# A chunked linear-attention layer: half of the product with V moved between the projections of k and v, all masks put ahead of the root, and the last step's gate taken in halves with another root

## The reference

```
xn = layernorm(x)
q, k, v = silu(xn Wq), silu(xn Wk), silu(xn Wv)
# lightning attention in chunks, D = exp(ld * lag) where lag >= 0
scores  = (q k^T) * D
o       = scores v + (q S) * q_decay
S_new   = chunk_decay * S + (k * k_decay)^T v
# gate and norm over each head of 16
o       = o * sigmoid((xn Wg1) Wg2)
o       = o * rsqrt(mean(o*o over the head) + 1e-5) * norm_w
s       = o Wo
g       = silu(fp8(xn * scale) fp8(W2 * scale1) / (scale * scale1))
out     = x + s * g
```

## Time and profile before

| | |
|---|---|
| median of 3 runs | 127.22 us (126.68 to 128.17) |
| the profiled execution's own time | 126.63 us |
| its span in the profile | 124.9 us |
| TensorE busy | 114.0 us (91%) |
| VectorE, ScalarE, GpSimd busy | 97.6, 85.1, 89.8 us |
| granted TensorE clock | full speed in all 40 slices |

### The profile page before, as it was taken

One profiled execution on the slowest core, in us unless ns is written; L12 is line 12 of the kernel. 1 busy time (PEld: TensorE's weight loads), 2 busy tenths in 40 slices (PEclk: granted clock), 3 DMA queues, 4 the chain that ended last, 5 costly groups with the idle time before them and its releaser, 6 DMA issues.

```text
span 124.9 us, 6418 instructions
## 1 busy us (share of the span) xinstructions
PE 114.0 (91%) x2694; PEld 100.2 (80%) x2694; DVE 97.6 (78%) x263; ACT 85.1 (68%) x163; POOL 89.8 (72%) x124
## 2 busy tenths in 40 slices
PE   3969989998999999999999899999999999896890
PEld 3969989867988899779987698889988998774770
DVE  1799999999895999759894968689956993395862
ACT  7589989989996757666776576685874486831200
POOL 6826599979999796949968894969692988240440
PEclk9999999999999999999999999999999999999999
DMA  2669910011000400042002400051004214000213
GB/s 85 201 179 295 327 40 3 5 26 26 5 5 8 82 0 5 0 94 84 0 8 54 119 5 5 8 136 32 5 5 97 76 18 116 5 5 5 78 49 127
DMA packets 11084, 7.57 MB, mean 61 GB/s; under 512 B 4848, under 2 KB 11056, under 8 KB 11056
## 3 DMA queue, kind: packets, MB, share of 16 engines
q1 hardware_dynamic: 11056, 7.17, 20.9%
HBM read 3.50 MB, written 2.10 MB: 45 GB/s over the span
## 4 chain that ended last, share of the span: by engine, by line
PE 69%; DVE 16%; issue 5%; ACT 4%; DMA 3%; SPq 1%; DVEq 0%
PE b_o L1281 8%; PE b_q L1113 5%; PE b_s L1211 5%; PE b_kv L1126 5%; PE b_kv L1127 5%; PE b_kv L1129 5%; PE b_q L1343 3%; PE b_o L1261 3%; PE b_kv L1192 3%; PE b_q L1235 3%; DMA ld_row<-in_L_attn_log_decay_dram 3%; PE b_x L1305 2%; PE b_q L1118 2%; PE b_s L1182 2%; PE b_s L1166 2%
## 5 line engine op out<-in xcount | busy, mean ns | idle before, releaser
L1126 PE MATMUL b_kv<-w_hi,xT_hi 128*128 128x256 f32 x64 | 16.6, 283 | 0.0
L1127 PE MATMUL b_kv<-w_lo,xT_hi 128*128 128x256 f32 x64 | 16.4, 280 | 0.0
L421 POOL TENSOR_TENSOR e_sum<-e_y,e_magic 128x512 f32<-128x512 f32 x8 | 10.3, 1288 | 8.0 <-DVE e_magic L784 7.8
L833 DVE SCALAR_TENSOR_TENSOR og<-gate_tanh,b_o 128x512 f32<-128x512 f32 x7 | 4.8, 686 | 12.2 <-PE b_o L1281 12.2
L459 POOL TENSOR_TENSOR y<-sg,x_sb 128x512 f32<-128x512 f32 x7 | 9.0, 1291 | 6.6 <-DVE sg L932 6.6
L1129 PE MATMUL b_kv<-w_hi,xT_lo 128*128 128x256 f32 x64 | 12.7, 280 | 0.0
L1281 PE MATMUL b_o<-probs,v_par 64*32 64x64 f32 x896 | 12.4, 223 | 0.0
L1126 PEld LDWEIGHTS b_kv<-w_hi,xT_hi 128*128 128x128 f32 x64 | 12.1, 189 | 0.2 <-issue 0.2
L1127 PEld LDWEIGHTS b_kv<-w_lo,xT_hi 128*128 128x128 f32 x64 | 12.1, 189 | 0.0
L470 POOL TENSOR_TENSOR on_lo<-on,on_hi 128x512 fp32r<-128x512 f32 x6 | 7.7, 1281 | 5.8 <-ACT on_hi L651 5.8
L426 POOL TENSOR_TENSOR e_q<-e_sum,e_magic 128x512 bf16<-128x512 f32 x8 | 10.8, 1348 | 0.5
(11 more groups left out here) (211 smaller groups left out, 378.7 us busy)
## 6 DMA issues: line engine op xcount, KB each, us to landing
out_dram<-y SPq DMA_DIRECT2D x7, 256.0 KB, 2.8
x_sb<-in_L_attn_x_dram SPq DMA_DIRECT2D x4, 384.0 KB, 6.0
own_cross<-own_end SPq DMA_DIRECT2D x12, 64.0 KB, 2.3
qd_cross<-qd SPq DMA_DIRECT2D x12, 64.0 KB, 2.3
x_sb<-in_L_attn_x_dram SPq DMA_DIRECT2D x2, 128.0 KB, 2.1
w_f<-in_L_attn_Wq_dram SPq DMA_DIRECT2D x1, 256.0 KB, 3.5
w_f<-in_L_attn_Wk_dram SPq DMA_DIRECT2D x1, 256.0 KB, 3.7
x_sb<-in_L_attn_x_dram SPq DMA_DIRECT2D x1, 256.0 KB, 4.2
```

Of the source, the lines that this page charges most:

```text
L421: g.tensor_tensor(e4_sum[:], e4_y[:, n % 2], e4_magic[:, n % 2], ALU.add).then_inc(s_e4sum, 1)
L1126: t.matmul(dst[:, s], xT_hi[:, u, kk, tok], w_hi[:, w, kk], start=(s == 0 and kk == 0), stop=False, skip_group_check=True)
L1127: t.matmul(dst[:, s], xT_hi[:, u, kk, tok], w_lo[:, w, kk], start=False, stop=False, skip_group_check=True)
```

## The change

Full steps. On TensorE, `from_chunk(n, 0, 0)` and `(n, 0, 1)` stand between `project_k` and `project_v`; `gate` stands ahead of `state_steps`; `from_chunk(n, 1, 0)` stands right behind `state_steps`. In step 6, `project_o(5, 0)` moves behind `state_steps(7)`. On VectorE, all three masks stand ahead of the root. On GpSimd, `mask_copy` is the first of the step. On ScalarE, `copy_scores` stands ahead of `normalise`, `square_w` behind `silu_q_parity`, and `high_on` behind `silu_v` and `gate`.

Last step. `gate_o` and `square_o` work in halves of the columns, and `head_sums` follows the halves. `product(5)` stands ahead of the gate. The root of step 7 is (s*s + v) / (u * s), with s the square root from ScalarE and u and v two forms of the mean square; it takes three VectorE instructions where there were four, and two small GpSimd instructions beside them. The blocks of the root are written in halves, and `keep_warm(2, ...)` ahead of `spread_blocks` is gone.

The diff, cut to its core:

```diff
             for n in range(1, STEPS - 1):
+                mask_copy(n)
                 sum_y(n + 1)
                 round_y(n + 1)
-                mask_copy(n)
                 decay_q(n + 1)
...
+
+            pool.wait_ge(s_sqrt, 3)
+            g.tensor_tensor(root_square[:], root_sqrt[:, 1], root_sqrt[:, 1], ALU.mult).then_inc(s_rootsq, 1)
+            pool.wait_ge(s_rootsq, 1)
+            pool.wait_ge(s_sqrt, 4)
+            g.tensor_tensor(root_num[:], root_square[:], root_var[:, 1], ALU.add).then_inc(s_rootnum, 1)
             add_x(STEPS - 2)
...
+            def square_o_last(half):
+                n = STEPS - 1
+                act.wait_ge(s_oglast, half + 1)
+                act.wait_ge(s_sum, n)
+                cols = slice(half * P, half * P + P)
+                a.activation(og_sq[:, :, cols], og[:, n % 2, :, cols], ACT.Square, scale=SQ_LAST).then_inc(s_sqlast, 1)
...
+            def square_root_last(n):
+
+                act.wait_ge(s_sum, n + 1)
+                a.activation(root_sqrt[:, n % 2], ps_sum_last, ACT.Sqrt, bias=root_eps[:, 1:2], scale=2.0 / E / SQ_LAST ** 2).then_inc(s_sqrt, 1)
+                act.wait_ge(s_lastrs, 5)
+                a.activation(root_var[:, n % 2], ps_sum_last, ACT.Identity, bias=root_eps[:, 1:2], scale=2.0 / E / SQ_LAST ** 2).then_inc(s_sqrt, 1)
...
                 nxt = known(n + 1)
+                copy_scores(n)
                 if known(n + 2):
                     normalise(n + 2)
-                copy_scores(n)
                 if nxt:
                     silu_q(n + 1)
                     high_g1(n + 1)
+                    silu_q_parity(n + 1)
                     square_w(n - 1)
-                    silu_q_parity(n + 1)
                     silu_k(n + 1)
...
                     find_over(n + 1)
-                    high_on(n - 1)
                     silu_v(n + 1)
                     gate(n + 1)
+                    high_on(n - 1)
...
+            def root_last(n):
+
+                u = n % 2
+                dve.wait_ge(s_sqrt, 3)
+                v.scalar_tensor_tensor(out=rs_half, in0=ps_sum_last, scalar=2.0 * E * EPS * SQ_LAST ** 2, in1=root_sqrt[:, u],
+                                       op0=ALU.add, op1=ALU.mult).then_inc(s_lastrs, 1)
+                dve.wait_ge(s_lastrs, 5)
+                v.reciprocal(rs_err, rs_half).then_inc(s_lastrs, 1)
+                dve.wait_ge(s_lastrs, 6)
+                dve.wait_ge(s_rootnum, 1)
+                v.scalar_tensor_tensor(out=root_y, in0=root_num[:], scalar=-(2.0 * E / 3.0) * SQ_LAST ** 2, in1=rs_err,
+                                       op0=ALU.mult, op1=ALU.mult).then_inc(s_lastrs, 1)
...
             for n in range(1, STEPS - 1):
-                mask(n, 2)
-                mask(n, 3)
+                for r in (2, 3, 0):
+                    mask(n, r)
                 root_seed(n - 1)
                 root_step(n - 1)
                 root_cubic(n - 1)
                 low_g1(n + 1)
                 root_full(n - 1)
                 root_pair(n - 1)
-                mask(n, 0)
                 head_norm(n - 1)
...
+            def head_sums_last():
+                pe.wait_ge(s_probs, masks(STEPS - 1))
+                for half in range(KH):
+                    pe.wait_ge(s_sqlast, half + 1)
+                    for s in range(S):
+                        mm = sums_of(ps_sum_last, half, s)
                 mm.then_inc(s_sum, 1)
...
                 project_k(n + 1, 0)
                 project_k(n + 1, 1)
+
+                from_chunk(n, 0, 0)
+                from_chunk(n, 0, 1)
                 project_v(n + 1, 0)
                 project_v(n + 1, 1)
                 spread_rs(n - 1)
-
+                gate(n + 1)
                 state_steps(n)
-                from_chunk(n, 0, 0)
-                gate(n + 1)
+                from_chunk(n, 1, 0)
                 if known(n + 2):
                     transpose_x(n + 2)
-                from_chunk(n, 0, 1)
-                from_chunk(n, 1, 0)
                 transpose_k(n + 1)
-                project_o(n - 1, 0)
+                if known(n + 2):
+                    project_o(n - 1, 0)
                 ffn(n + 1)
                 from_state(n)
                 from_chunk(n, 1, 1)
                 if not known(n + 2):
                     state_steps(n + 1)
+
+                    project_o(n - 1, 0)
                 else:
                     project_o(n - 1, 1)
```

110 lines of the change are left out of this document (67 added, 43 removed).

## The result

The changed kernel takes 129.1 us (median of four runs, 128.57 to 129.78) against 126.95 us of the kernel before on the same chip: 2.2 us between the medians. The prediction was 130.0 and slower. The profiled execution took 128.57 us with a span of 126.9, which is 2.0 us more than before.

The account below looks back on a forecast made before the run. TensorE, busy 114.0 of 124.9 us, was taken as the bound, without slack in full steps. Steps 1 to 5 +2.3, step 6 +0.9, last step -0.4 make +2.8 on 127.22: 130.0 us, range 126.9 to 131.5.

Parts of the forecast that it names:

- The wait of the transposes: Full steps: TensorE's transpose_k waits for VectorE's state end, 0.6 us a step (0.5 to 0.7), 0.4 in step 1.
- The two waits lie beside each other and are not added.: Full steps: transposes' wait for the state and scores' wait for the ffn's silu overlap; both say 13.7 us a step.
- Steps 2 and 4: Step 2: its 0.5 us TensorE idle time falls into the new wait, leaving +0.1; step 4 pays +0.6 in full.
- "faster" rival: Late TensorE instructions are the larger cost and the change relieves them; over 1% faster if the wait is hidden too; chance 0.11.
- The sum of steps 1 to 5: Full steps: +0.4 in step 1, +0.1 in step 2, +0.6 each in steps 3 to 5; together +2.3 us.
- Step 6: Later on_hi delays GpSimd's on_lo, own_mid and kd, so from_state and state_steps(7) wait: +0.9 us.
- Last step: Halves, new root and moved product(5) let the last norm start earlier: -0.4 us, bounds 0 and -0.6.
- the case's low end: Whole kernel: lowest time of the main case, 128.8 us, the case running to 131.4.
- The rule and the row: Skill page's mostly hidden instruction crossings give +3.3 us in sum; step 2's idle row, read as late instructions, gives +2.8.

Follow-up runs that it names:

- experiment 6: Changed kernel with TensorE's gate behind state_steps again and ScalarE's on_hi ahead of the tanh: 128.38 us, 1.014 of the kernel before.
- experiment 7: Changed kernel with gate behind state_steps, on_hi ahead of the tanh, kT and the ffn's silu ahead of e_y: 127.82 us, 1.010 of the kernel before.
- experiment 5: Changed kernel with ScalarE doing kT and the ffn's silu ahead of e_y: 128.39 us, 1.014 of the kernel before.
- experiment 1: Changed kernel with its full steps put back as before on all four engines, last step's edits kept: 126.01 us, 0.996 of the kernel before.
- experiment 9: Kernel before with 64 more 32 by 32 matmuls (each became two) in the prologue, to shift TensorE's instruction stream: 133.92 us in one execution.
- Experiment 8: Changed kernel with GpSimd's own_mid and kd ahead of on_lo, in step 6 alone: 128.95 us, 1.018 of the kernel before.
- experiment 4: Changed kernel with TensorE's full steps in the order of before, project_o(5, 0) still moved, other engines as changed: 132.28 us, 1.047 of the kernel before.
- experiment 12: Kernel before with the last step's halves and new root, and project_o of step 5 moved behind state_steps(7): 126.10 us, 0.996 of the kernel before.
- experiment 10: Changed kernel with the last step's og and its square as one instruction each, new root kept: 129.86 us, 1.025 of the kernel before.

## Why the prediction was right, and where its steps were not

**The wait of the transposes.** Right in cause, place and number: five waits for `state_end`, and experiments 6 and 7 take them away. Predicted 0.6 us each and 0.4 in step 1; the list shows 0.49 and 0.31 of idle time, and with the 0.13 by which a start precedes its predecessor's modelled end, 0.62 from where the transposes would have started.

**"The two waits lie beside each other and are not added."** This failed by a little. Steps 3 and 5 grew by 0.85 and 0.66 us, not 0.6. The scores' wait for the ffn's silu came on top with 0.13 us (experiment 5; experiment 7 shows that the two add), and splitting k from v costs 0.18 us that I had priced at nothing, 0.09 of them given back because the gate stands with the wide matmuls.

**Steps 2 and 4.** +0.1 was predicted for step 2 and +0.20 measured: the stall of 0.5 was indeed covered for the most part. For step 4 I counted +0.6 and it lost nothing, because its stall of 0.83 was 0.04. I can't put that down to the change: the four kernels with its full steps as they are have 0.00 to 0.09 us there, but experiment 1, with the full steps of before, has 0.08 as well, and experiments 5 and 7, with the product in its new place, 0.59 and 0.41. The size goes with when one instruction packet ends (experiment 9), which no row that I had could tell. So the late instructions of my "faster" rival are a real cost, but that the new order relieves them is shown in step 2 alone, where they fall into the wait. The sum of steps 1 to 5, +2.26 against +2.3, is right because these errors cancel, and that was luck.

**Step 6.** Predicted +0.9 by way of `on_hi`, `on_lo`, `own_mid`; measured +0.92. Experiment 8 gives 0.59 of it back by GpSimd's order alone; 0.34 of the rest is a wait of the `ffn` matmuls for `xqT` that I had not named.

**Last step.** From the product's end to the end -0.38 us was measured (10.56 to 10.18) for -0.4 predicted, but the shares were wrong: 0.46 from the halves, 0.2 from the root, and 0.2 lost again ahead of it, where I had counted a gain of 0.1 for the moved `product(5)`. GpSimd's small instructions held VectorE 0.32 us, not 0.15. What failed is that the step stopped there: with the full steps changed, the stretch between the last step's scores and the product's end got 0.8 us shorter, for its stalls, and no term had it. TensorE's order alone doesn't do that: experiments 4 and 12 have the same TensorE program from the first to the last instruction, and this stretch takes 5.45 us in one and 6.28 in the other. It makes the profile's +2.0 out of the predicted +2.8.

**Sums and readings.** With 0.5 us a wait and -0.6 in the last step the case's low end is 130.0 - 0.5 - 0.2 = 129.3 us, not 128.8; the measured 129.1 lies 0.2 under it, inside the stated range of 126.9 to 131.5 all the same. GpSimd's instructions of 2 columns take 0.25 to 0.75 us in the trace of before, not 0.2; the 0.3 us taken for 64 columns was right (0.29 and 0.32). Between the second and third call of the product stand 16 wide matmuls, not 24.

**The rule and the row.** By the Trainium skill (Runtime: NRT & Kernel Launch, Instruction fetch mechanics), with the crossing hidden and the product's place indifferent, the sum was +3.3; by the row of step 2 it was +2.8. They differ in step 2 alone, +0.6 against +0.1, and it measured +0.20: the row's side. The crossings cost 2.8 us in the kernel before by the reading of experiment 9, so here they are not hidden at four places. The profile's +2.0 lies under both sums, for the stalls above.

## What to carry to other kernels

When an engine has no slack, count for each moved piece the first consumer on every other engine and what is queued behind it: here the matmuls cost about 0.1 us a step to move, and 2.4 us of the loss are a state update that came 1.2 us later, a copy that stood behind a tanh, and two multiplications behind it. Look also for the wait that is second in line: removing the first alone gave 0.22 us a step, the second alone 0.13, both 0.34. And before a gain or loss in one step is put down to an edit, look for a kernel without the edit in which that step moved too: step 4's stall went from 0.83 to 0.08 us with no edit ahead of it. An order moved on one engine can't be tested alone where the others were moved with it: two such kernels were 2.5 to 2.7% slower than the changed kernel, which they were meant to mend.

## What the hardware showed that I had not expected

TensorE's stalls without a releaser were 0.1 to 1.1 us of idle time, all at the same four places of its stream in 14 traces, and each ended 1.3 to 1.8 us behind the end of an instruction packet. Their sum was 2.8 us in the kernel before, 0.6 in the changed one (0.13, 0.04 and 0.40) and 3.2 in experiment 9, with the same matmuls in the steps; that is over 1% of the time, and in step 4 it changed by 0.75 us with no edit ahead of it. In the one execution with 128 small matmuls in the prologue the clock fell to its lower level, 1.2 GHz, for 6 us, and the prologue took 6.9 us longer, 4.8 of them the small matmuls themselves; that they are what lowered the clock is not shown. Halving a 0.63 us ScalarE instruction and the one before it saved 0.46 us on the path (experiment 10): the squares start 0.46 us behind the start of `og`, where they started 0.77 us behind it, so the engines overlap over the halves.
